# First MLP layer as single fp32 matmuls, whole array tiles, one set of DMAs on another queue and a new order in a windowed-attention block

## What is computed

```python
xn  = (xw - mean) * rsqrt(var + eps) * g + b          # over the 96 channels of a token
q, k, v = split(xn @ qkv_w.T + qkv_b)                 # 12 heads of 8
attn = softmax(q * SCALE @ k.T + bias[head])          # 49 x 49 in each window and head
out  = (attn @ v) @ proj_w.T + proj_b
seq  = x + out
seq2 = batchnorm(depthwise_conv3x3(seq))
h    = gelu(seq2 @ w1.T + b1)                         # 96 -> 384
y    = seq2 + h @ w2.T + b2                           # 384 -> 96
```

## Time and profile before

| | |
|---|---|
| median of 3 runs | 3448.92 us (3444.31 to 3459.77) |
| the profiled execution, its own time | 3444.23 us |
| its span, first to last instruction | 3442.4 us |
| busy share PE / DVE / ACT / POOL | 90% / 89% / 82% / 58% |
| granted TensorE clock, mean | 0.992 |
| mean DMA rate | 84 GB/s |

### The profile page before, as it was taken

The page is one execution under the profiler, slowest core; times in us unless marked ns, Lnnn a source line. Parts: engine busy times, 40 slices in busy tenths (PEclk is TensorE's granted clock), DMA queues, the critical chain, the costliest instruction groups (busy, mean ns, idle before and its releaser), DMA issues.

```text
span 3442.4 us, 213611 instructions
## 1 busy us (share of the span) xinstructions
PE 3098.5 (90%) x94988; PEld 2172.5 (63%) x94988; DVE 3071.3 (89%) x4907; ACT 2833.2 (82%) x4883; POOL 1999.8 (58%) x2574
## 2 busy tenths in 40 slices
PE   3899989989989889899899898999998998998996
PEld 2666666666666666666666666666666666666663
DVE  4889989989989889899899898999998998999995
ACT  3888888878888888888888888888888888888885
POOL 2565656656656556566565565565655665656654
PEclk9999999999999999999999999999999999999998
DMA  1232322323323223233232233232322332322321
GB/s 38 81 91 80 91 87 84 91 81 89 90 80 92 86 84 89 81 88 88 82 89 85 86 88 88 86 89 86 91 82 86 87 88 84 88 86 87 90 84 35
DMA packets 269976, 289.20 MB, mean 84 GB/s; under 512 B 55651, under 2 KB 252580, under 8 KB 269062
## 3 DMA queue, kind: packets, MB, share of 16 engines
q1 hardware_dynamic: 236294, 198.40, 20.7%
q0 software_dynamic: 32768, 77.14, 6.5%
HBM read 39.34 MB, written 38.54 MB: 23 GB/s over the span
## 4 chain that ended last, share of the span: by engine, by line
PE 75%; DVE 11%; issue 8%; POOL 4%; ACT 1%; SPq 0%; POOLq 0%; DMA 0%; ACTq 0%; DVEq 0%
PE d_ps L256 22%; PE b_ps L256 16%; PE a_ps L256 12%; PE sm_ps L315 8%; PE st_ps L294 8%; PE o_ps L340 8%; DVE s L739 5%; POOL sl L631 2%; DVE mx L713 2%; DVE y L776 1%; POOL sh L624 1%; DVE kl L747 1%; DVE ql L747 1%; DVE ximg L795 1%; POOL ox L615 0%
## 5 line engine op out<-in xcount | busy, mean ns | idle before, releaser
L739 DVE SCALAR_TENSOR_TENSOR s<-ximg,cols,s 96x392 f32<-96x392 f32 x1792 | 1351.3, 754 | 44.1 <-POOL s L604 7.8
L713 DVE TENSOR_REDUCE mx<-sm_ps 128x12 f16<-128x588 f32 x1024 | 778.8, 761 | 57.1 <-PE sm_ps L315 53.0
L600 POOL TENSOR_TENSOR s<-ximg,cols 96x392 f32<-96x392 f32 x256 | 216.3, 845 | 969.9 <-DVE y L776 969.7
L468 ACT ACTIVATE p<-st_ps 128x588 f32<-128x588 f32 x1024 | 672.0, 656 | 82.7 <-PE st_ps L294 45.5
L315 PEld LDWEIGHTS sm_ps<-k_all,q_all 127*49 127x49 f16 x24576 | 493.5, 104 | 306.3 <-issue 228.9
L256 PE MATMUL d_ps<-g,w_s 128*64 128x392 f32 x3072 | 671.2, 506 | 3.6 <-ACT g L519 2.7
L615 POOL DMA_DIRECT2D ox<-o_sb x1024 | 582.6, 572 | 36.2 <-ACT o_sb L493 16.5
L294 PE MATMUL st_ps<-q_all,k_all 128*49 128x49 f16 x24576 | 541.1, 185 | 61.9 <-issue 56.9
L294 PEld LDWEIGHTS st_ps<-q_all,k_all 128*49 128x49 f16 x24576 | 479.4, 103 | 181.0 <-issue 97.6
L315 PE MATMUL sm_ps<-k_all,q_all 127*49 127x49 f16 x24576 | 526.6, 186 | 53.4 <-issue 48.9
L340 PE MATMUL o_ps<-p,v 128*32 128x49 f32 x24576 | 400.6, 210 | 33.5 <-issue 31.7
(11 more groups left out here) (114 smaller groups left out, 6122.4 us busy)
## 6 DMA issues: line engine op xcount, KB each, us to landing
ox<-o_sb POOLq DMA_DIRECT2D x1024, 73.5 KB, 2.3
k_all<-kh SPq DMA_DIRECT2D x512, 75.0 KB
q_all<-qh SPq DMA_DIRECT2D x512, 75.0 KB
x_sb<-in_x SPq DMA_DIRECT2D x256, 147.0 KB, 2.7
out<-y SPq DMA_DIRECT2D x256, 147.0 KB
k_all<-kl SPq DMA_DIRECT2D x256, 75.0 KB
q_all<-ql SPq DMA_DIRECT2D x256, 75.0 KB
q_all<-mxt SPq DMA_DIRECT2D x256, 9.4 KB, 2.0
```

What stands on the lines that cost most here:

```text
L468: af(p32[:, p, :, :].rearrange("p (b h) n -> p b h n", b=2), st_ps[:, :, 0:HALF].rearrange("p b (h n) -> p b h n", n=TOK), ACT.Exp).then_i ...
L713: v.tensor_reduce(mx[:, c % 2, :, p].rearrange("p (b h) -> p b h", b=2), sm_ps[:, :, 0:HALF].rearrange("p b (h n) -> p b h n", n=TOK), AX. ...
L739: v.scalar_tensor_tensor(acc, image_rows(c, k // 3, k % 3), cw_c[:, k:k + 1], acc, ALU.mult, ALU.add)\
```

## The change

- `hidden`: one fp32 matmul of 128 weight columns on `w1_s` and `s2` in place of six f16 halves. The f16 parts `w1_h`, `w1_l`, `sh`, `sl`, their set-up, and POOL's `image_high` and `image_low` are gone. `hidden` waits for tap 8.
- `centred` and `variance`: one fp32 matmul of 96 weight columns in place of two halves of 64. `values`: three matmuls of 128 weight columns for each window pair in place of six (`whole_three`). Queries, keys, projection and the second layer stay in halves.
- `to_channels`, four DMAs of 73.5 KB, goes from POOL's queue to SP's.
- PSUM banks change hands: keys in `d_ps`, values, `hidden` 0 and the second layer in `b_ps`, the variance and `hidden` 2 in `a_ps`.
- All five loops are written anew, with one step more (`STEPS = CHUNKS + 9`). `outputs(c, 1)` waits for `values_times_p(c, 3)`.

```diff
+            def whole_three(o, sh, sl, mh, ml):
+                mm(o, sh, mh, start=True, stop=False)
+                mm(o, sh, ml, start=False, stop=False)
+                return mm(o, sl, mh, start=False, stop=True)
 # centred
-                halves(d_ps[0:128, 0:CT], center[:, :], x_sb[:, at:at + CT]).then_inc(xc_done, 1)
+                mm(d_ps[0:C, 0:CT], center[:, 0:C], x_sb[:, at:at + CT], start=True, stop=True).then_inc(xc_done, 1)
 # hidden
-                    wait(pe, sl_done, c)
+                    wait(pe, tap_done[8], c)
-                halves_three(hidden_ps[k][:, 0:CT], w1_h[...], w1_l[...], sh[:, :], sl[:, :]).then_inc(hid_done[k], 1)
+                mm(hidden_ps[k][:, 0:CT], w1_s[:, k * 128:(k + 1) * 128], s2[0:C, c % 2, :], start=True, stop=True).then_inc(hid_done[k], 1)
 # PE's loop, after
+                values(s - 3)
+                max_scores(s - 3, 3)
+                exp_scores(s - 4, 1)
+                projection(s - 6)
+                exp_scores(s - 4, 2)
+                maxima_rows(s - 3)
+                values_times_p(s - 4, 0)
+                hidden(s - 8, 0)
+                hidden(s - 8, 1)
+                hidden(s - 8, 2)
+                second(s - 8, 0)
+                exp_scores(s - 4, 3)
+                second(s - 8, 1)
+                max_scores(s - 2, 0)
+                keys(s - 1)
+                queries(s - 1)
+                second(s - 8, 2)
+                max_scores(s - 2, 1)
+                values_times_p(s - 4, 1)
+                centred(s)
+                exp_scores(s - 3, 0)
+                values_times_p(s - 4, 2)
+                max_scores(s - 2, 2)
+                variance(s)
+                values_times_p(s - 4, 3)
 # ACT's loop, after
+                inverses(s - 5)
+                exp(s - 4, 3)
+                outputs(s - 4, 0)
+                square(s)
                 exp(s - 3, 0)
                 outputs(s - 4, 1)
+                log_variance(s)
                 exp(s - 3, 1)
+                root(s)
                 exp(s - 3, 2)
                 act.preload_act_table_set("gelu_and_others")
                 gelu(s - 7, 0)
                 input_high(s)
                 gelu(s - 7, 1)
                 gelu(s - 7, 2)
-                outputs(s - 3, 0)
                 act.preload_act_table_set("natural_log_exp_and_others")
-                exp(s - 3, 3)
+                log_sums(s - 4)
                 key_high(s)
                 query_high(s)
 # DVE's loop, after
+                tap(s - 7, 4)
+                tap(s - 7, 5)
                 maxima(s - 2, 0)
+                key_low(s - 1)
                 block_out(s - 8)
+                query_low(s - 1)
                 maxima(s - 2, 1)
+                tap(s - 7, 6)
+                normalise(s - 5)
                 tap(s - 7, 7)
+                maxima(s - 2, 2)
+                values_out(s - 2)
                 tap(s - 7, 8)
+                maxima(s - 2, 3)
                 tap(s - 6, 2)
                 input_normal(s)
                 maxima_out(s - 2)
                 image_sum(s - 5)
                 tap(s - 6, 3)
 # POOL's loop, after
+                first_tap(s - 6)
                 input_low(s)
 # SP's loop, after
+                load(s)
+                term(q_all, 1, qh, qh_done, s - 3)
+                to_channels(s - 6)
+                maximum_row(s - 4)
+                first_term(k_all, 2, kh, kh_done, s - 2)
+                term(k_all, 0, kh, kh_done, s - 2)
+                term(k_all, 1, kl, kl_done, s - 2)
                 term(q_all, 2, ql, ql_done, s - 2)
+                store(s - 9)
                 term(q_all, 0, qh, qh_done, s - 2)
```

More of the change, by code:

```diff
@@ L227, in maximum_row, with to_channels @@
                              mxt[:, c % 2, :, :].rearrange("m w t -> m (w t)")).then_inc(row_in[c % 2], 16)
+            def to_channels(c):
+                if not real(c):
+                    return
+                wait(sp, proj_done, c - 2)
+                wait(sp, o_done[0], c)
+                wait(sp, o_done[1], c)
+                for x4 in range(4):
+                    sp.dma_start(ox[:, c % 2, x4, :], o_sb[x4::4, c % 2, :, :]).then_inc(o_in[c % 2], 16)
             def store(c):
@@ L356, in variance @@
                 wait(pe, sq_done, c)
-                free(pe, (kl_done, c-1), (g_done[2], c-8), (g_done[0], c-8), (lnv_done, c-1))
-                halves(b_ps[0:128, 0:CT], avg[:, :], sq[:, :]).then_inc(var_done, 1)
+                free(pe, (ql_done, c-1), (g_done[2], c-8), (sum_done, c-6), (lnv_done, c-1))
+                mm(a_ps[0:C, 0:CT], avg[:, 0:C], sq[:, :], start=True, stop=True).then_inc(var_done, 1)
             def queries(c):
@@ L417, in second @@
                 wait(pe, g_done[k], c)
-                if k == 1:
-                    free(pe, (g_done[1], c+0), (xn_done, c+7), (y_done, c-1))
-                halves(d_ps[0:128, 0:CT], w2_s[:, k, :], g[:, k, :], start=k == 1, stop=k == 0).then_inc(s_done[k], 1)
+                if k == 0:
+                    free(pe, (g_done[0], c+0), (v32_done, c+5), (y_done, c-1))
+                halves(b_ps[0:128, 0:CT], w2_s[:, k, :], g[:, k, :], start=k == 0, stop=k == 2).then_inc(s_done[k], 1)
             for s in range(STEPS):
+                values(s - 3)
[19 more added lines that the diff above has]
+                exp_scores(s - 3, 0)
                 values_times_p(s - 4, 2)
-                centred(s)
                 max_scores(s - 2, 2)
-                exp_scores(s - 3, 1)
-                values(s - 2)
                 variance(s)
[L429 to L447, removed]
+                values_times_p(s - 4, 3)
         @block.scalar
@@ L489, in outputs @@
                     return
-                wait(act, pv_done[1 if half == 0 else 2], c)
+                wait(act, pv_done[1 if half == 0 else 3], c)
                 if half == 0:
@@ L604, in first_tap @@
                 tt(acc, acc, one, ALU.add).then_inc(tap_done[1], 1)
[L606 to L630, removed]
-                tt(sl[:, :], s2[0:C, c % 2, :], sh[:, :], ALU.subtract).then_inc(sl_done, 1)
             for s in range(STEPS):
-                image_low(s - 7)
-                to_channels(s - 4)
+                first_tap(s - 6)
                 input_low(s)
-                first_tap(s - 5)
-                image_high(s - 6)
         @block.vector
```

69 lines of the change are left out of this document (21 added, 48 removed).

## The result

The kernel after takes 3739.44 us in the median of its runs (3736.37 to 3743.24), the kernel before 3446.78 us (3444.31 to 3459.77); the ratio is 1.085, with a 95% interval of 1.083 to 1.087. So it is slower by 8.5%. The profiled execution took 3739.95 us, its span is 3738.2 us.

A forecast was written before the change was run, and what follows sets the result against it. PE was taken to bound the kernel before at 12.96 us per chunk; after, PE's sum gave 13.7 and the ring 13.84. So 3444.2 + 225 + 5 = 3674 us, range 3430 to 3790.

The forecast's parts named there:

- The ring: Loop from DVE's maxima 2 over PE and ACT back to maxima 2, lasting one period: 13.84 us with POOL's turns.
- The walk's first step: From the end of DVE's maxima 2 over PE's max 3 and exp 1 to ACT's start of exp 1: 0.95 us.
- PE's sum: PE's period of 12.96 us per chunk plus added terms, less the stops that go: 13.7.
- ACT's part: ACT from exp 1 to key_high without any wait: 7.12 us, so kh is ready at 8.07.
- The borders of whole tiles: On PE, 128-column work next to 64-column work at four new places, 0.11 us each: +0.44 per chunk.
- The relief: PE's stops with nothing to wait for ("issue") shrink as matmul and load records go: -0.3 us per chunk.
- POOL's parts: PE's wait for POOL's sl and sh goes: -0.4 us per chunk, bounds 0 and 0.54.
- Values: On PE, twelve matmuls with 128-column loads in place of twelve pairs: +0.1 us per chunk.
- Edits at nothing: to_channels on SP's queue, POOL's lost work, the smaller set-up and the later outputs 1 wait: no cost expected.
- Rival A: Faster: instruction stalls go altogether, whole tiles are no mode of their own; PE's sum 12.4, 3300 us; chance 0.14.
- Rival B: PE alone, mild: POOL's turns fall elsewhere and whole tiles are free; 13.2, thus 3510 us; chance 0.23.
- Rival C: Weight loads of whole tiles are not hidden on PE: 15.4 to 16.9, about 4050 to 4450 us; chance 0.05.

The follow-up runs named there:

- two experiments that rested on a single leg: Kernel after with log_sums put behind query_high on ACT, 3735.55 us; the same with halves everywhere as well, 3737.43 us.
- the first experiment: Kernel after with hidden, centre, variance and values in halves of 64 columns again, hidden still fp32: 3736.95 us, ratio 1.084.
- one part alone: Kernel before with centre, variance and values alone in whole tiles: 3383.64 us, ratio 0.980.
- another: Kernel before with only the first MLP layer in whole fp32 tiles, POOL's image_high and image_low gone: 3725.26 us, ratio 1.080.

## Why the prediction was right, and where not

The direction, the size and the mechanism held: 3674 us forecast, 3739 measured, inside 3430 to 3790.

- **The ring.** Predicted 13.84, measured 14.10 (and 14.12 in the turn shown). PE idle before max 3 for DVE's `mx`, DVE idle before `kl` for `kh`, tap 6 at 1.13, the transpose wait gone: all as written; `normalise` is at 1.37 where 1.2 to 1.3 was. (The walk's first step, 0.95, comes to 0.91 by its own terms; 0.92 was measured.) Removing POOL's turns took 165 us off, and returning to halves took nothing, which parts the ring from PE's sum.
- **The step that was mis-sized** is ACT's part, "From there ACT waits for nothing". The scores of exp 2 use the same two PSUM banks as those of exp 1 and may start only when ACT has read exp 1: PE's projection starts at 1703.09 and exp 2 at 1704.01, 0.92 where 0.66 is its cost, and ACT starts exp 2 0.70 behind root instead of 0.42. `kh` comes at 8.33 instead of 8.07; from there to the end of `maxima 2` it is 5.79 where 5.77 was forecast. 0.26 x 256 = 67 us is the whole gap between 3674 and 3740.
- **One leg, or two.** The walk took `block_out` to be ready when `key_low` let it start. It was, but by no more than 0.1 us (the 0.06 above), and so a second leg of the same length went unnoticed. It does not change the forecast, but two experiments that rested on a single leg missed.
- **PE's sum, 13.7, was 0.4 too high, by errors that partly cancel.** PE without its wait for `maxima 2` is at 14.10 - 0.78 = 13.3. The pace of a whole fp32 block (0.66) and of a single `values_times_p` group (0.40, and some 0.1 to enter) were right. Three terms were too low, by some 0.6: hidden 2.18 - 1.50 = 0.68 where 0.48 and a border of 0.11 were forecast (its end is in part a wait for gelu); the variance 0.09 on entry (1713.46 to 1713.89 against 0.34) and 0.83, where 0.11 and 0.66 were; and the transpose now sits between exp 2 and `values_times_p 0`, 0.67 from exp 2's start where a group takes 0.34, which no term held. The borders of whole tiles were too high, 0.23 net by the first experiment where 0.44 was taken. The relief was too low: "issue" went from 0.86 per chunk to nothing, where 0.3 was taken. POOL's parts were taken too high: PE's waits before have only 31.1 us, 0.12 per chunk, on POOL's `sl`, where 0.4 was read from the chain's share. The view of waits does not name every stop, either. In the kernel before the median distances between PE's records add up to 11.6 per chunk, so stops of every kind were 1.4 of the 12.96, twice the relief of 0.7, and the additions were 1.7 where 1.44 was summed.
- **Values.** Twelve loads of 128 columns cost nothing beside the border: 1700.96 to 1701.43 is eleven steps of 0.043, the pace of the pairs of halves too. The +0.1 was not there.
- **Edits at nothing.** The move to SP's queue was one, by the run that makes it alone.
- **Rival A** was right that the stops go altogether, and wrong that this decides the change: in the new order the ring had taken over. Nor was it the smaller number of records that ended them at 14.1, since in halves they stay away too (7.4 us); at 13.5 it may count, with 4.9 us in whole tiles and 66.1 in halves (there with `log_sums` moved too). Rival B falls with `normalise` at 1.37. Rival C falls with the 0.66 of the middle block. The Trainium skill's rule on weight loads and row groups (TensorE: Matmul & The Clock Gate, The mechanism) is not what these rows show: a whole fp32 block costs as much as one in halves. The same section of the Trainium skill also lets a load run ahead when it goes to the background weight buffer, and with that these rows agree. The Trainium skill's rule that a change of tiling mode drains TensorE (TensorEngine Tiling (Array Packing), Key Properties) agrees with borders that cost 0.09 to 0.20 each in the old order.

## What to carry to other kernels

When every engine has slack and the period is still longer than any sum of work, follow one chunk from engine to engine until the walk comes back to its start, and count every single-buffered tile on the way as an edge. Before moving an operation to another form, count what it adds at its borders and what it takes off the instruction stream, and put the parts of a large change into the old order one at a time: here one part alone was worth 2% and another cost 8%. A wait that looks idle can be what keeps two engines out of each other's turns.

## What the runs showed of the hardware

- DVE operations with two SBUF inputs and POOL operations take turns of a whole operation: `normalise` 1.37 against 0.55, tap 6 1.13 against 0.61, and POOL's own multiplies 1.16 against 0.84 beside taps. The Trainium skill has this as an exclusive lock (SBUF — State Buffer, SBUF: two separate sides), and the trace agrees. What I had not expected is how much hangs on the phase: the same 3 us of POOL work per chunk, released from its wait, gained one order 4.4% and cost the other 6.4%.
- Stops of PE with nothing to wait for fell from 220.7 to 57.5 us with 4.3% fewer matmul records. A fall in proportion to the records would have been 9 us. The same 93452 records went with 244.1 us of stops in the old order and with 66.1 (period 13.5) and 7.4 (period 14.1) in the new one: their number alone does not set the stops.
- A border between matmuls of 128 and of 64 or fewer weight columns costs 0.09 to 0.16 us on entering and 0.16 to 0.20 on leaving in the old order, and less in the new one, where the neighbours differ (centre 0.83 in whole against 0.71 in halves, for both of its borders). Entering 32-column groups costs some 0.1. Loads of 128 columns, fp32 or f16, in a run of such matmuls are hidden.
